# Attention and routed experts on one core: attention scores in four groups of 32 rows, and where routing and expert weights are handled

## What is computed

```python
x = x + xattn(layernorm(x), ctx)     # 16 heads of 16: softmax(q k^T / 4) v, then @ Wo.T + bo
n = layernorm(x)
e = argmax(n @ router_w.T + router_b)                        # one of 32 experts for each token
x = x + relu(relu(n @ w1[e] + b1[e]) @ w2[e] + b2[e])        # 256 -> 64 -> 256
```

## Time and profile before

| | |
|---|---|
| Median of three runs | 2137.03 us (2135.17 to 2138.63) |
| Profiled execution, first to last instruction | 2137.2 us |
| PE busy | 1898.6 us (89%) |
| DVE busy | 1553.0 us (73%) |
| ACT busy | 1209.9 us (57%) |
| POOL busy | 604.0 us (28%) |
| Mean granted clock of TensorE | 0.880 |

### The profile page before, as it was taken

One profiled execution on the slowest core, in us unless ns is written; L12 is line 12 of the kernel. 1 busy time (PEld: TensorE's weight loads), 2 busy tenths in 40 slices (PEclk: granted clock), 3 DMA queues, 4 the chain that ended last, 5 costly groups with the idle time before them and its releaser, 6 DMA issues.

```text
span 2137.2 us, 51280 instructions
## 1 busy us (share of the span) xinstructions
PE 1898.6 (89%) x18624; PEld 1418.2 (66%) x18624; DVE 1553.0 (73%) x4242; ACT 1209.9 (57%) x2241; POOL 604.0 (28%) x532
## 2 busy tenths in 40 slices
PE   3699998989898989898989989898999399999998
PEld 2577776767676767676767767676777266666665
DVE  4488888878888888788878888888887444444443
ACT  2476666667666667666766666666667022222222
POOL 4112222222232222222222222222310134444444
PEclk8799999999999999999999999999999655555555
DMA  7800000111111110001000000011000333333320
GB/s 267 280 21 32 32 31 32 36 35 33 32 41 32 41 32 31 32 31 32 31 32 32 32 32 31 32 39 35 31 11 12 85 100 100 100 100 99 98 72 22
DMA packets 64060, 119.28 MB, mean 56 GB/s; under 512 B 8433, under 2 KB 45692, under 8 KB 63614
## 3 DMA queue, kind: packets, MB, share of 16 engines
q1 hardware_dynamic: 44734, 60.65, 9.5%
q0 software_dynamic: 19072, 55.15, 7.4%
HBM read 60.65 MB, written 59.31 MB: 56 GB/s over the span
## 4 chain that ended last, share of the span: by engine, by line
PE 63%; DVE 21%; issue 11%; POOL 3%; DMA 1%; DVEq 0%; SPq 0%; POOLq 0%; another core or an unknown queue 0%; ACT 0%
PE sc L812 13%; PE sc L988 9%; PE b L980 8%; PE b L826 6%; DVE mx L492 5%; DVE work L558 5%; PE sc L810 5%; PE b L773 4%; PE b L833 4%; PE b L973 3%; PE sc L791 3%; PE b L847 3%; PE b L782 2%; DVE rz L534 2%; DVE st L549 1%
## 5 line engine op out<-in xcount | busy, mean ns | idle before, releaser
L385 ACT ACTIVATE qM<-qT,cst 128x512 fp32r<-128x512 f32 x1024 | 640.0, 710 | 0.0
L812 PE MATMUL sc<-qM,kT 128*128 128x512 f32 x1536 | 518.8, 432 | 0.0
L310 POOL DMA_INDIRECT pages<-row,slot_i x128 | 129.0, 1008 | 1183.5 <-DVE slot_i L635 1151.1
L395 ACT ACTIVATE pv<-sc 128x512 f32<-128x512 f32 x512 | 295.6, 594 | 127.1 <-PE sc L812 122.0
L492 DVE TENSOR_REDUCE mx<-sc 128x4 bf16<-128x512 f32 x512 | 318.0, 684 | 53.1 <-issue 39.3
L812 PEld LDWEIGHTS sc<-qM,kT 128*128 128x128 f32 x1536 | 254.5, 193 | 16.5
L343 POOL DMA_INDIRECT out<-work x160 | 193.2, 1207 | 237.0 <-DVE work L725 234.2
L810 PEld LDWEIGHTS sc<-mxT,sel_b 128*128 128x128 bf16 x2048 | 116.7, 98 | 172.9 <-issue 124.1
L810 PE MATMUL sc<-mxT,sel_b 128*128 128x128 bf16 x2048 | 204.9, 223 | 25.1 <-DVE mxT L529 25.0
L534 DVE RECIPROCAL rz<-b 128x256 f32<-128x256 f32 x128 | 223.7, 1748 | 0.7 <-PE b L826 0.7
L988 PE MATMUL sc<-xs,rz 65*128 65x256 f32 x320 | 195.2, 714 | 0.0
(11 more groups left out here) (119 smaller groups left out, 3158.7 us busy)
## 6 DMA issues: line engine op xcount, KB each, us to landing
pages<-empty POOLq DMA_DIRECT2D x8, 2600.0 KB, 23.2
work<-pages SPq DMA_DIRECT2D x40, 520.0 KB, 3.9
xs<-x_in SPq DMA_DIRECT2D x32, 512.0 KB, 3.5
work<-ctxT SPq DMA_DIRECT2D x32, 512.0 KB, 3.3
out<-work POOLq DMA_INDIRECT x160
pv<-w SPq DMA_DIRECT2D x1, 2080.0 KB
w1s<-w SPq DMA_DIRECT2D x1, 2064.0 KB
pages<-row,slot_i POOLq DMA_INDIRECT x128
```

What stands on the lines that cost most here:

```text
L385: ins = act.activation(qM[:, u % 2, :, :, h, :], qT[:, par, :, :, u * P:(u + 1) * P].bitcast(F32), ACT.Copy, scale=cst[:, C_MASK + h:C_MAS ...
L395: act.activation(pt[:, u % 2, j], sc[j][:, :], ACT.Exp).then_inc(S["exp_out"], 1)
L812: ins = pe.matmul(sc[j][:, :], kT[:, par, a, c, u * P:(u + 1) * P], qM[:, u % 2, b, c, 4 * (j % 2):4 * (j % 2) + 4, :].rearrange("p h t -> ...
```

## The change

- **Scores.** Q is stored twice (a mask each for even and odd heads) instead of eight times, and Q and K are plain fp32 without a low part. A product takes 32 rows of the array, and the four groups of rows, each with a PSUM bank of its own, are issued one after another: 8 fp32 products of 256 columns for a batch. The 16 products for the maxima and the 16 that subtract it take 32 rows each too, two groups of rows alternating.
- **Maxima in halves.** The products for the maxima go into two banks `mb`, two groups of rows at a time; the second half is issued at the end of the batch before, when DVE has reduced the first half.
- **Values and sums.** V has 16 columns of ones beside each head's 16, so that one product gives both: 16 fp32 products instead of 32. DVE transposes the result in 32 x 32 blocks, takes 16 reciprocals, multiplies, and transposes back.
- **Engines.** Both norms go from DVE to ACT, as do the copies of V; the bias of V is folded into the output's. ACT takes the logits, which are now made transposed by products of 32 columns. Argmax becomes two reductions and three elementwise operations on DVE. Page slots and the row's token and expert go to POOL (some 25 small operations for a group), which also gets two more for each norm.
- **Expert weights.** The first weights stay in HBM: SP reads a page's expert number and loads 66 KB for each page into a ring of eight. The second weights stay in one table in SBUF, filled up with zeros to 128 rows, and PE reads the number and takes its operand from there. Both products now use 128 rows x 128 columns of the array. DVE's two copies go.
- **Start and end.** SP, not POOL, fills the pages with empty rows: 40 pages early, four more with each group. Every `step` spans three groups before and three after, with rings of four for x and the rows.

The diff, cut to its core (lines that begin with a blank are context):

```diff
-            def masks(q, par, u, at):
...
-                for h in range(8):
-                    ins = act.activation(qM[:, u % 2, :, :, h, :], qT[:, par, :, :, u * P:(u + 1) * P].bitcast(F32), ACT.Copy,
-                                         scale=cst[:, C_MASK + h:C_MASK + h + 1])
+            def proj_copy(q, par, n):
+                after(act, "proj_done", 4, q, n)
+                c = n % 2
+                if n < 2:
+                    ins = act.activation(kT[:, par, c], pA[:, :], ACT.Identity, bias=bk_s[:, c:c + 1])
+                else:
+                    for m in range(2):
+                        ins = act.activation(qM[:, par, m, c], pA[:, :], ACT.Identity,
+                                             scale=cst[:, C_MASK + m:C_MASK + m + 1], bias=bqm[:, m, c:c + 1])
+                ins.then_inc(S["proj_out"], 1)
...
+            def scores_for_max(par, u, half_):
+                for j in range(4):
+                    for i in range(2):
+                        g, m, c = 2 * half_ + i, j // 2, j % 2
+                        rows = slice(32 * g, 32 * g + 32)
+                        ins = pe.matmul(mb[i][:, j * P:(j + 1) * P], qMh[rows, par, m, c, u * P:(u + 1) * P],
+                                        kTh[rows, par, c, u * P:(u + 1) * P], start=True, stop=True)
+                ins.then_inc(S["S_done"], 1)
...
+            def scores(par, u):
+                for c in range(2):
+                    for g in range(4):
+                        rows = slice(32 * g, 32 * g + 32)
+                        dst = sc[g][:, :].rearrange("p (m c t) -> p c m t", m=2, c=2)[:, c]
+                        pe.matmul(dst, kT[rows, par, c, u * P:(u + 1) * P], qM[rows, par, :, c, u * P:(u + 1) * P],
+                                  start=(c == 0), stop=False, skip_group_check=True)
+
+            def subtract_max(q, u):
+                after(pe, "mxT_out", 4, q, u)
+                for pair in ((0, 1), (2, 3)):
+                    for j in range(4):
+                        for g in pair:
+                            rows = slice(32 * g, 32 * g + 32)
+                            ins = pe.matmul(sc[g][:, j * P:(j + 1) * P], sel_b[rows, j, :], mxT[rows, :],
+                                            start=False, stop=True, skip_group_check=True)
...
+            def attend(par, b, u):
+                for j in range(4):
+                    for g in range(4):
+                        h = 8 * (j % 2) + 2 * g + j // 2
+                        ins = pe.matmul(pB[32 * g:32 * g + 32, j * P:(j + 1) * P], vs[:, par, u, h, :], pt[:, b, g, j, :],
+                                        start=True, stop=True)
+                ins.then_inc(S["PV_done"], 1)
...
+            def normalise(q, u):
+                after(dve, "PV_done", 4, q, u)
+                dve.transpose(tr[:, :], pB[:, :]).then_inc(S["tr_out"], 1)
...
+                dve.reciprocal(inv[:, :], tr[:, :].rearrange("p (k r) -> p k r", r=32)[:, :, HD]).then_inc(S["inv_out"], 1)
...
+                dve.transpose(aT[:, :, :].rearrange("p c t -> p (c t)"), nrm[:, :]).then_inc(S["aT_out"], 1)
...
+            def load_w1(n, r, first):
+                if not first:
+                    apart(sp, ("h_out", n - (W1R - 1)))
+                e = sp.value_load(table[0:1, bass.ds(n, 1)], min_val=0, max_val=E - 1)
+                sp.dma_start(w1p[:, r % W1R, 0:2 * HID + 1],
+                             w1[:, bass.ds(e, 1), :].rearrange("p e h -> p (e h)")).then_inc(S[f"w1_in{r % W1R}"], 16)
...
             def page_norm(n, r):
-                e = dve.value_load(table[0:1, bass.ds(n, 1)], min_val=0, max_val=E - 1)
-                dve.tensor_copy(w1p[:, r % PN, :], w1s[:, bass.ds(e, 1), :].rearrange("p e h -> p (e h)"))
-                dve.tensor_copy(w2p[:, r % PN, :], w2s[:, bass.ds(e, 1), :].rearrange("p e d -> p (e d)"))
...
             def page_first(n, r):
+                pe.wait_ge(S[f"w1_in{r % W1R}"], (n - r % W1R) * (16 // W1R) + 16)
...
-                    ins = pe.matmul(bank[0:HID, 0:P], w1p[:, r % PN, i * HID:(i + 1) * HID], pnT[:, r % 2, i * P:(i + 1) * P],
+                    ins = pe.matmul(sc[2 + r % 2][:, 0:P], w1p[:, r % W1R, i * HID:i * HID + P], pnT[:, r % 2, i * P:(i + 1) * P],
...
             def page_second(n, r, first):
+                e = pe.value_load(table[0:1, bass.ds(n, 1)], min_val=0, max_val=E - 1)
...
-                pe.matmul(sc[r % 4][:, 0:D], hT[:, r % 2, :], w2p[:, r % PN, :], start=True, stop=True).then_inc(S["y_done"], 1)
+                pe.matmul(mid[r % 4][:, 0:D], hT[:, r % 2, :], w2s[:, bass.ds(e, 1), :].rearrange("p e d -> p (e d)"),
+                          start=True, stop=True).then_inc(S["y_done"], 1)
```

1152 lines of the change are left out of this document (554 added, 598 removed).

## The result

The changed kernel takes 1337.31 us (median of 4 runs, 1336.46 to 1339.77); the kernel before takes 2137.83 us beside it. The ratio is 0.626, with a 95% interval of 0.625 to 0.627.

A forecast was written before the change was run, and what follows sets the result against it. PE was taken to bound both attention and the page loop. Start and hand-over 88, attention 128 x 8.67 = 1110, pages 160 x 1.8 = 288 and 14 for first load and end sum to 1500 us, range 1356 to 1650.

The forecast's parts named there:

- That keeps the waits of before: Attention: the 8.67 us batch leaves PE's waits unchanged; some 0.6 us on the second norm may go, lower end 8.05.
- The price of a change of shape: Attention: each switch in how PE's array is used costs 0.14 us; three more per batch add 0.4 us.
- I take 1.8: Page loop: 1.8 us a page at 2.4 GHz, ends 1.4 and 2.4; 160 pages make 288 us.
- the 2.4 us of nothing hidden: Page loop: upper end for a page if the array's work hides nothing of PE's number reading and issuing.
- Hand-over: Between attention and page loop: stays near 40 us because the same chain runs once more; 38 us taken.
- Pages at 1.2 GHz: Rival, page loop: the clock does not rise, 160 x 0.6 = +96 us, 1596 us in all; chance 0.25.
- Weight loads that do not overlap: Rival, attention: 16 fp32 loads take 1.88 instead of 0.94 us, +120 us, 1620 us in all; chance 0.14.
- Row groups one after another: Rival, attention: no overlap, 12.3 us a batch, +468, 1968 us; chance 0.10, shared with DVE's transposes at their upper end.
- Slower through the clock in attention: Rival: PE runs attention at 1.2 GHz, 15.8 us a batch, pages 2.4 us, 2508 us in all; chance 0.05.
- Its low end: Whole kernel: 8.05 us a batch and 1.4 us a page, 88 + 1030 + 224 + 14 = 1356 us.
- 8.7 us: Sign, attention: distance between equal pieces of two neighbouring groups, over four, is 8.7 us.
- 0.9 to 1.2 us for the score rows: Sign, attention: the 16 score rows take 0.9 to 1.2 us, starting in fours a few ns apart.

The follow-up runs named there:

- the first way of doing it: Changed kernel with bookkeeping copies between GpSimd's second and third scatters, bias addition between third and fourth: 1428.67 us against 1466.01 unedited; later also part of three edits together, 1391.94 us.
- the first trace: Profile of the unedited changed kernel from its first comparison with the kernel before, without the stall: 1337.31 us median, profiled span 1334.6 us.
- the last chip: Chip without the stall: the kernel of three edits (scatters apart, one load moved, longer loop body) took 1329.16 us, with no two scatters neighbouring 1321.11 us.

## Why the prediction was wrong, point by point

**What bounds before, and what the change does to it: right.** PE set both parts. The scores run four groups at a time; the clock stayed at 0.99 in attention and rose in the page loop; no other engine became the bound of attention at a price near its upper end (transposes 0.72 and 0.45 us where 0.62 and 0.42 were taken and up to 5.2 was feared; POOL 54% busy in attention, small operations 0.2 to 0.46 us where 0.4 was taken).

**Attention, -123 us.** The step that failed is "That keeps the waits of before". PE's idle time fell from 1.18 to 0.70 us a batch: -0.48 us, 61 us in all. The prediction saw that 0.6 us of it hung on the second norm on VectorE, and used this only for its lower end. The norm went to ACT, where it takes 0.6 us for 256 columns and the wait is 0.5 us a batch; the turns of the hardware loop are nearly all of the rest. The other 0.48 us are PE's busy time, 7.49 forecast, 7.01 measured:
- the subtraction, taken two rows at a time (0.46 us), runs in all four groups at once: 0.23;
- the scores and half of the maxima's products run beside each other instead of one after the other. The prediction added up its terms as if one followed the other; terms on different row groups overlap. Its second failed step is this sum. How the remaining 0.25 us divide between this overlap and smaller terms was not measured.

The price of a change of shape held: 0.14 us taken, 0.16 measured.

**Page loop, -53 us.** The step that failed is "I take 1.8". The clock was right. The floors were all named in the prediction: 1.07 for the streams, 1.28 for POOL, 1.33 for PE with its reading, near 1.4 for SyncE. The value was put above all of them, between their highest and the 2.4 us of nothing hidden, with no row behind the difference. Measured: SyncE 1.46, the highest floor, and the loop at 1.50. The loads of first weights are what fills SyncE: with one in four on another queue a page falls from 1.87 to 1.72 us, and to 1.40 us where nothing stalls.

**Hand-over, +15 us.** The chain of the changed kernel there, longest pieces (start, length):

```profile
1047.52 1.12 POOL pages L370
...
1059.38 1.10 POOL pages L370
...
1071.00 1.10 POOL pages L370
...
1081.55 5.28 DMA arena<-w
```

The last three groups come through routing one behind the other, 11.6 to 11.9 us apart, since the chain of small operations is now on GpSimd, with the scatters on the same queue; and behind the scatters come the table, the pages and then the first weights, whose load takes 5.3 us until it lands. The prediction said that "the same chain of norm, router, slots and scatters runs once more", and did not price its move from VectorE to GpSimd there, where nothing covers it.

**The rivals.** Pages at 1.2 GHz: did not come, but both products narrow give it at once, 2.61 us a page. Weight loads that do not overlap: PE weight loads are busy 686 of 987 us in attention and hidden. Row groups one after another: no. Slower through the clock in attention: no, 0.99.

**The range.** Its low end joined the low ends of two terms and left hand-over and everything else at the forecast. It allowed 8.05 us a batch because PE's busy time was held for sure; that was the term that was never given a lower bound. Two of its sums are a little off: 8.67 less 0.6 is 8.07, not 8.05, and the rival of row groups one after another comes to +466 us, not +468. Neither matters.

**What would show it.** "8.7 us" for a batch wrong (7.9 inside the hardware loop); "0.9 to 1.2 us for the score rows" right (their starts span 0.92 us), but they start in pairs, 0.05 us and more apart, not in fours; clock right; "1.8 us a page" wrong; transposes below 0.8 right; POOL under 75% right.

## What to carry to other kernels

When a change frees the engine that sets the time, price its waits as well as its work: ask of each wait what it hung on and whether that thing is itself being moved. For a loop near several floors, forecast the highest floor, and add to it only what a row shows; here that would have given 1.46 instead of 1.8. A kernel that leans on another queue in tight runs (four scatters behind each other) can differ by 10% between chips while its predecessor differs by less than 0.5% (its medians); run it on more than one before trusting a few per cent. Taking such runs apart helped where the stall was, but the first way of doing it cost 0.5 us a group where it was not. And look at an edit's effect batch by batch: a mean of 0.46 us was 0.8 in two batches and nothing in another.

## What was not expected of the hardware

- **The stall at the scatters.** On four chips, in the changed kernel, whatever waits for TensorE is held while GpSimd issues four scatters in a row: 28 times in a run, 76 us on VectorE's transpose alone. With only two scatters as neighbours this wait shrinks from 2.7 to 0.66 us. The stall is absent in the first trace and on the last chip, and the kernel before does not have it on one of the four. It reaches SyncE too: its register instructions, at most 0.19 us long without the stall, take up to 0.7 us. So TensorE alone is not the cause. What is, stays open: no experiment tells the queues, the signals between engines and the chip apart.
- **Row groups go ahead of each other.** Rows of the scores start 0.03 us after the first of the maxima's and 0.04 us before the next six, which were issued ahead of them; and the subtraction's 16 rows take 0.23 us though they are issued for two groups first and then for the other two.
- **A turn of the hardware loop** costs PE 2.77 us of standing still and some 3 us at 0.50; three fewer gave 11.0 us.
- **The clock of the page loop** has no single cause in the shape: with either product narrow (one run each) it stays as high as in the untouched loop or within 0.05 of it, with both it stays at 0.50 at full load.
- **Moving four transposes by 1 us of queue** cost 1.6 us in a batch without the stall.
